# A store of its own for each group of turned columns: seven stores a tile in place of three

## The reference

```python
center = einsum('nchw,oc->nohw', feature, w_center)
step = relu(einsum('nchw,oc->nohw', feature, w_step))
prob = sigmoid(einsum('nchw,oc->nohw', feature, w_prob))
offset = transpose(center * step, (0, 2, 3, 1))
th = minimum(round(gh + offset[..., 0]), h - 1)
tw = minimum(round(gw + offset[..., 1]), w - 1)
tgt = mod((th * w + tw).reshape(n, h * w).astype(int32), h * w)
sample = vmap(lambda idx: grid_flat.at[idx].set(grid_flat))(tgt)
sampled = grid_sample_bilinear(feature, normalised(sample))
proped = sampled * prob + feature * (1.0 - prob)
out = feature * prob + proped * (1.0 - prob)
```

## The kernel before, in words

| sweep | mixes | writes table | computes indices |
|---|---|---|---|
| 0 | no | 0 | no |
| 1 | no | 1 | of unit 0 |
| 2 | unit 0 | 2 | of unit 1 |
| 3 | unit 1 | 3 | of unit 2 |
| 4 | unit 2 | no | of unit 3 |
| 5 | unit 3 | no | no |

## Time and profile before

### The profile page before, as it was taken

How to read it: one execution, slowest core, us unless ns; L and a number is a source line. 1 busy time by engine, 2 the same in 40 slices (tenths; PEclk the granted TensorE clock), 3 DMA queues, 4 the chain that set the end, 5 groups by cost and what they waited for, 6 DMA issues and landing times. The chain is left out here.

```text
span 7465.5 us, 92049 instructions
## 1 busy us (share of the span) xinstructions
PE 5108.6 (68%) x26404; PEld 2886.7 (39%) x26404; DVE 5269.5 (71%) x12387; ACT 3045.9 (41%) x5830; POOL 4128.5 (55%) x8124
## 2 busy tenths in 40 slices
PE   5763554346765677568957666679957646788888
PEld 3442333223443444345634334335533223344444
DVE  7538577267776643777789963778889964687777
ACT  3442222222232333222302323767706647566666
POOL 6657653446363464554506426765516436677776
PEclk8876776677887888789978877889979878899999
DMA  7995666667586888676715778776606566787887
GB/s 279 348 341 181 219 214 217 205 208 248 185 279 204 280 291 288 222 234 220 266 38 205 242 244 272 214 205 196 194 18 186 167 148 209 231 253 256 260 263 233
DMA packets 543222, 1672.98 MB, mean 224 GB/s; under 512 B 125182, under 2 KB 180339, under 8 KB 501012
## 3 DMA queue, kind: packets, MB, share of 16 engines
q1 hardware_dynamic: 223708, 827.34, 35.8%
q10 hardware_dynamic: 254552, 763.42, 27.2%
q0 software_dynamic: 64480, 76.57, 5.5%
HBM read 949.39 MB, written 727.71 MB: 225 GB/s over the span
## 5 line engine op out<-in xcount | busy, mean ns | idle before, releaser
L1103 DVE TENSOR_TENSOR ps<-ps,arena 128x400 f32<-128x400 f32 x1600 | 927.8, 580 | 1409.1 <-PE ps L1293 859.2
L1049 POOL TENSOR_TENSOR arena<-arena 128x32 f32<-128x32 f32 (+8 forms) x3013 | 973.7, 364 | 1537.2 <-PE ps L1319 1528.7
L1283 PE MATMUL ps<-arena,minus 128*128 128x400 f32 x3200 | 1600.1, 585 | 240.1 <-DVE arena L1105 226.6
L1422 ACT ACTIVATE arena<-ps 128x400 f32<-128x400 f32 x1600 | 798.0, 499 | 2185.2 <-PE ps L1269 1037.0
L1333 PE MATMUL ps<-ident,arena 128*128 128x128 f32 x5000 | 906.5, 328 | 840.9 <-ACT arena L1397 529.4
L1249 POOL DMA_INDIRECT arena<-table,gidx x800 | 887.3, 1109 | 697.3 <-PE ps L1302 457.5
L1397 ACT ACTIVATE arena<-ps 128x512 f32<-128x512 f32 (+1 forms) x1400 | 734.6, 552 | 1231.6 <-PE ps L1333 608.5
L1333 PEld LDWEIGHTS ps<-ident,arena 128*128 128x128 f32 x5000 | 737.2, 203 | 1026.3 <-ACT arena L1397 618.7
L1302 PE MATMUL ps<-arena 128*64 128x400 f32 x3200 | 767.6, 559 | 468.6 <-ACT arena L1436 197.9
L1293 PEld LDWEIGHTS ps<-ident,arena 100*128 100x128 f32 x6400 | 768.4, 150 | 640.6 <-issue 474.6
L1249 POOL DMA_INDIRECT arena<-table,arena x800 | 820.6, 1026 | 268.4 <-issue 239.4
(11 more groups left out here) (214 smaller groups left out, 5859.5 us busy)
## 6 DMA issues: line engine op xcount, KB each, us to landing
arena<-x SPq DMA_DIRECT2D x200, 1600.0 KB, 10.8
arena<-table SPq DMA_DIRECT2D x400, 800.0 KB
table<-arena ACTq DMA_DIRECT2D x400, 512.0 KB, 5.1
y<-arena ACTq DMA_DIRECT2D x200, 800.0 KB, 9.1
arena<-y SPq DMA_DIRECT2D x100, 1600.0 KB, 14.2
out<-arena ACTq DMA_DIRECT2D x200, 800.0 KB
table<-arena ACTq DMA_DIRECT2D x200, 576.0 KB, 10.5
conv<-arena ACTq DMA_DIRECT2D x800, 31.2 KB
```

Source lines behind the costliest of these rows:

```text
L1049: last = E.tensor_tensor(tmp[:, :, at:at + size], cols[:, :, y + to:end + to:step], cols[:, :, y:end:step], ALU.subtract)
L1103: V.tensor_tensor(d, d, g, ALU.mult).then_inc(s_mix, 1)
L1283: nc.tensor.matmul(ps[:, sums(r), 0:W], minus[:, :], tile(t)[:, r * W:(r + 1) * W], start=True, stop=False)
L1422: nc.scalar.activation(gate[m % 2], ps[:, 6 + m % GB, 0:W], ACT.Copy).then_inc(s_gcopy, 1)
```

## The change

Each of the seven groups is a piece of its own, so a tile has seven stores: six of 2048 bytes a partition and one of 512. The buffers t_out shrink from nine columns of 128 words to four (T_WORDS is computed from PIECES), and there are four of them in mixing sweeps and eight in input sweeps. Each has its semaphore. Nothing else is changed: the turns, the copies out of PSUM, their order and the bytes written are the same.

```diff
-PIECES = [(0, 2), (2, 4), (4, 7)]
+PIECES = [(g, g + 1) for g in range(7)]
...
         T_WORDS = max(TURNED[b - 1][0] + TURNED[b - 1][1] - TURNED[a][0] for a, b in PIECES) * CH2
-        t_out = [part(T_WORDS) for _ in range(2)]
+        t_out = [part(T_WORDS) for _ in range(4)]
...
-        t_out += [again(rows_at[0] + BROWS * NFIX + a * T_WORDS, T_WORDS) for a in range(2)]
+        t_out += [again(rows_at[0] + BROWS * NFIX + a * T_WORDS, T_WORDS) for a in range(4)]
...
-        s_tst = [sem(f"s_t_st{a}") for a in range(4)]
-        counts = {"f": [0] * 4, "rows": [0] * 3, "y": [0] * 4, "t": [0] * 4}
+        s_tst = [sem(f"s_t_st{a}") for a in range(8)]
+        counts = {"f": [0] * 4, "rows": [0] * 3, "y": [0] * 4, "t": [0] * 8}
...
-            TR, CR = 2 if mixing else 4, len(c_out)
+            TR, CR = 4 if mixing else 8, len(c_out)
```

More of the change, by code:

```diff
@@ L246, in build @@
         T_WORDS = max(TURNED[b - 1][0] + TURNED[b - 1][1] - TURNED[a][0] for a, b in PIECES) * CH2
-        t_out = [part(T_WORDS) for _ in range(2)]
+        t_out = [part(T_WORDS) for _ in range(4)]
         htmp = [part(W) for _ in range(NEARBY[-1])]
         wtmp = [part(BROWS * NFIX).rearrange("p (r n) -> p r n", n=NFIX)]
-        t_out += [again(rows_at[0] + BROWS * NFIX + a * T_WORDS, T_WORDS) for a in range(2)]
+        t_out += [again(rows_at[0] + BROWS * NFIX + a * T_WORDS, T_WORDS) for a in range(4)]
         htmp += [again(conv_at - (a + 1) * W, W) for a in range(2)] + gate
-        assert BROWS * NFIX + 2 * T_WORDS + 2 * W <= 2 * STRIPS * HALF * CH2
+        assert BROWS * NFIX + 4 * T_WORDS + 2 * W <= 2 * STRIPS * HALF * CH2
         wtmp.append(again(rows_at[0], BROWS * NFIX).rearrange("p (r n) -> p r n", n=NFIX))
```

## The result

The changed kernel takes 7514.61 us (median of 16 runs, 7503.49 to 7537.01) against 7490.24 us (16 runs, 7474.54 to 7511.21) before: a ratio of 1.0032, interval 1.0020 to 1.0043. That is 24 us slower where 29 were forecast.

A forecast was written before the change was run, and what follows sets the result against it. It took DMA engines as full in the first input sweep and four mixing stretches, compute engines limiting elsewhere. Terms 15 + 13 + 5 - 4 = +29 us gave 7534 us on a 7504.9 us median; 8-in-10 range 7475 to 7590.

The forecast's parts named there:

- the likeliest case: The forecast itself: whole kernel 10 to 55 us slower, 7515 to 7560 us; chance 0.45.
- First sweep: First input sweep, 50 tiles: extra packets and ScalarE issues together cost 0.3 us a tile, 15 us (0 to 30).
- C: First input sweep: a tile's late last turn delays the next load into its buffer, at most 0.6 us a tile.
- Packets: Mixing sweeps' full DMA stretches, 42 tiles: 576 more packets a tile cost 0.3 us each tile, 13 us (0 to 16).
- Issues in the mixing sweeps: Other 58 mixing tiles: extra ScalarE issues mostly hide behind VectorE or TensorE; 5 us (0 to 103).
- the wait for a buffer: Mixing sweeps: ScalarE's first wait for a table store ends earlier, the last a little later; -4 us (-97 to +54).
- Sweep 1 costs nothing: Second input sweep: a longer tile is free, as ScalarE idles 80.23 us at its end while GpSimd's list finishes.
- The 92 full tiles: Tiles passing while DMA engines are taken as full: 50 in the first sweep, 42 in four mixing stretches.
- Hidden: Rival: packet and issue costs both vanish, whole kernel within 10 us, 7505 us; chance 0.23.
- Faster: Rival: shorter buffer waits release the mixing earlier, a quarter of 291.2 us gained, 7461 us; chance 0.19.
- Much slower: Rival: three buffer waits in turn, plus unhidden ScalarE issues, add 54 us in mixing sweeps, 7588 us; chance 0.12.
- A fixed time for each store, laid end to end: Rival: 1.1 us fixed for each of four more stores in 92 full tiles, 405 us, 7910 us; chance 0.01.

## Why the prediction was right

**Direction and size.** 29 us forecast, 24 measured, and the packets were counted to the packet. But the sum is right in part by cancelling, and in part by luck: the term of the first sweep was half of what came, and the terms of the mixing sweeps, which were to cost 14, come to 3 together with an interval that holds both 0 and 14. The time of 7534 us is 19 above the measured median, mostly because it stood on 7504.9 us, the median of three runs, where sixteen give 7490.24; for the same reason the time falls at the lower edge of the likeliest case's own range, 7515 to 7560. Term by term:

- **First sweep, 15 us (0 to 30).** Right in place, short by half: 31 us between profiles, 30 us by the ratio of the split in the input sweeps, at the upper bound. This is the term that was mis-sized. I worked out that four more stores put 2.4 us into a tile's burst on ScalarE, and then followed only the last turn that waits for one of them (C, which the four PSUM banks don't bear out). The queue as a whole should have been added up. Before, ScalarE worked, issued or stood within 0.13 us of either for 7.9 of 9.7 us a tile. The split puts 2.1 us on that, and what was free was 1.8: the queue runs full (10.0 of 10.4 us), and a tile gets 0.7 us longer. I also did not add the packets' 0.3 us to it. With the queue relieved in both kernels the split still costs 26 us by the dates, so the packets, or something else in the split that is not the queue's length, have a share; what share stays open.
- **Packets, 13 us in the mixing sweeps' full stretches.** 17 us by the run with packets alone, scaled; its interval and a difference of kernels in layout leave that rough. In the first sweep they show as 7 us (one trace), inside the scatter.
- **Issues in the mixing sweeps, 5 us, and the wait for a buffer, -4 us.** The split there comes to 3 us (-12 to +18) in all. With 17 for the packets, issues and waits together must come to about 3 - 17 = -14, with at least the 15 us of that interval to either side. That the small issues cost some 30 us behind the first sweep, and that waits can reach the end in the run with two buffers, speaks for both terms being larger than I took them and of opposite sign; no run separates them, so this is argued, not shown.
- **Sweep 1 costs nothing.** Between the profiles sweep 2's first mixing starts 36.6 us later and sweep 1 itself 32.1 us later, so its share is 4.5 us, within the scatter.
- **The 92 full tiles.** The first sweep's share of 0.94 was near the DMA engines' limit and near ScalarE's at once. In the four stretches of the mixing sweeps packets cost and shorter waits gave no gain that can be told, which is what full engines would do; nothing tests each stretch by itself.

**The rivals.** Hidden: 15 to 32 us by the interval of the ratio, so more than its 10. The DMA engines had some room (packets alone took the share from 0.94 to 0.97); ScalarE's queue had less than the split put on it. Faster: 96.6 us of waits vanished from ScalarE (291.2 to 194.6) without a gain that can be told. Much slower: three waits in turn did not add up through four buffers; through two, waits of this kind cost 313 us. A fixed time for each store, laid end to end: the 405 us of that rival were not there, and neither were the 1600 us that I estimated by the Trainium skill's "DMA: Bandwidth & Descriptors". Its section "Anatomy of one DMA — SWDGE (gpsimd) path" gives the 2 us for DMAs that GpSimd issues, while these stores are issued by ScalarE, so this case says nothing against the figure itself.

## What to carry to other kernels

Add up an engine's queue with its DMA issues and its waits for its own writes before calling it idle: 186 busy us of 400 were a full queue in one of six sweeps. When a transfer is split, price the issues on the queue that makes them, and the packets on the DMA engines, and compare each with the room that is left. Where two limits lie as close as here, relieving one uncovers the other: moving four other issues to SyncE's queue gave 21 us back, but it gave 14 to the kernel without the split too. So test a remedy on the kernel before as well, or its gain is taken for proof of the cause. And give each store its share of buffers: the same seven stores cost nothing that can be measured through four small buffers and 4% through two.

## What the runs showed of the hardware

- A packet costs about 10 ns of a DMA engine's time besides its bytes, by two routes: 10.2 ns from two windows of the earlier trace rows, and 1170 us for the 115,200 packets more (9 to 11 ns with the shares' rounding).
- Stores of 16 x 4 bytes, 800 in all, made the kernel 4% slower, and large transfers beside them too: 270 GB/s in the first sweep in place of 350. The same stores with 512 bytes in each partition made it 1% slower.
- The same four issues on ScalarE took 1.65 us in one kernel and 2.71 us in another that differs in two PSUM banks; why was not tested.
- The kernel before took 7484 to 7490 us on some chips and 7802 to 7805 us on others, 4% apart, at a mean granted TensorE clock of 0.835 and 0.820 of full speed.
